# Second norm's scale and shift stored beside the x1 rows, a reordered end of attention, and useless matmuls in the waits of the routing

## The reference

```python
x = x + tanh(g_xattn) * attn(layernorm(x), ctx, Wq, bq, Wk, bk, Wv, bv)   # softmax(QK^T) * 256**-0.5 @ V
h = layernorm(x)                                     # the second norm
e = argmax(h @ router_w.T)                           # one expert for each token
x = x + tanh(g_ffn) * ((silu(h @ gate[e].T) * (h @ up[e].T)) @ down[e].T)
```

## Time and profile before

| | us |
|---|---|
| median of 3 runs | 225.41 |
| lowest and highest of them | 222.13, 226.23 |
| the profiled execution's own time | 221.01 |
| its span, first to last instruction | 218.9 |
| TensorE busy in the span | 199.7 (91%) |
| ScalarE, VectorE, GpSimd busy | 109.8, 130.8, 136.1 |
| mean granted TensorE clock, 1 is 2.4 GHz | 0.96 |

### The profile page before, as it was taken

One profiled execution on the slowest core, in us unless ns is written; L12 is line 12 of the kernel. 1 busy time (PEld: TensorE's weight loads), 2 busy tenths in 40 slices (PEclk: granted clock), 3 DMA queues, 4 the chain that ended last, 5 costly groups with the idle time before them and its releaser, 6 DMA issues.

```text
span 218.9 us, 4538 instructions
## 1 busy us (share of the span) xinstructions
PE 199.7 (91%) x1200; PEld 170.9 (78%) x1200; DVE 130.8 (60%) x430; ACT 109.8 (50%) x223; POOL 136.1 (62%) x138
## 2 busy tenths in 40 slices
PE   7899999997665789999999999999999999999960
PEld 3667998985564678888888888888888888888850
DVE  2886899867699125537555537564636565645650
ACT  1478777664500534495269485369475444422410
POOL 3004099495473897339966998987998985212111
PEclk9999999999787589999999999999999999999996
DMA  6999315928600319621581085194003012011000
GB/s 208 340 394 378 135 49 163 368 73 291 217 0 0 99 25 358 211 68 38 189 313 32 0 311 189 34 383 126 1 8 92 0 51 68 9 49 51 5 28 20
DMA packets 11845, 29.43 MB, mean 134 GB/s; under 512 B 1986, under 2 KB 8517, under 8 KB 10790
## 3 DMA queue, kind: packets, MB, share of 16 engines
q1 hardware_dynamic: 6320, 20.20, 25.9%
q0 software_dynamic: 2064, 5.12, 7.8%
q10 hardware_dynamic: 3430, 3.74, 5.1%
HBM read 24.85 MB, written 4.72 MB: 135 GB/s over the span
## 4 chain that ended last, share of the span: by engine, by line
PE 83%; DVE 6%; ACT 3%; DMA 3%; issue 2%; ACTq 1%; POOL 0%; POOLq 0%; DVEq 0%
PE ps L929 36%; PE ps L941 12%; PE ps L908 6%; PE ps L944 5%; PE ps L790 3%; PE ps L729 3%; PE ps L770 3%; DMA both<-in_ctxT 3%; PE ps L811 3%; PE ps L759 2%; PE ps L901 2%; PE ps L800 2%; PE ps L750 2%; PE ps L878 1%; DVE V L1193 1%
## 5 line engine op out<-in xcount | busy, mean ns | idle before, releaser
L929 PE MATMUL ps<-wgu,xhT 128*128 x360 | 83.1, 384 | 1.2 <-DVE xhT L1229 1.2
L929 PEld LDWEIGHTS ps<-wgu,xhT 128*128 128x128 f32 x360 | 66.3, 191 | 12.5 <-issue 1.6
L464 POOL DMA_INDIRECT xin<-x_rows,table x23 | 22.7, 986 | 29.4 <-DVE xin L1264 21.5
L941 PE MATMUL ps<-wd,hT 128*128 x114 | 40.5, 392 | 0.0
L396 POOL TENSOR_TENSOR wgu<-raw_gu,wgu (+1 forms) x12 | 38.6, 3253 | 0.1
L1246 DVE TENSOR_TENSOR A<-xin,ps 128x512 f32<-128x512 f32 (+1 forms) x40 | 20.6, 520 | 25.4 <-ACT xin L656 14.6
L656 ACT ACTIVATE xin<-ps 128x512 f32<-128x512 f32 (+1 forms) x40 | 18.6, 465 | 31.5 <-PE ps L929 31.1
L469 POOL DMA_INDIRECT out<-xin,table x20 | 20.3, 1015 | 18.3 <-DVE xin L1264 13.2
L650 ACT ACTIVATE hT<-ps 128x512 fp32r<-128x512 f32 x20 | 11.8, 592 | 32.9 <-PE ps L908 32.9
L944 PE MATMUL ps<-wd,hT 128*128 x95 | 26.6, 280 | 0.0
L941 PEld LDWEIGHTS ps<-wd,hT 128*128 128x128 f32 x114 | 21.3, 187 | 3.9
(11 more groups left out here) (163 smaller groups left out, 310.7 us busy)
## 6 DMA issues: line engine op xcount, KB each, us to landing
raw_gu<-in_Wgu SPq DMA_DIRECT2D x8, 1408.0 KB, 6.5
both<-in_Wd SPq DMA_DIRECT2D x8, 640.0 KB, 4.3
x_rows<-x ACTq DMA_DIRECT2D x8, 256.0 KB, 3.4
xin<-in_x SPq DMA_DIRECT2D x7, 256.0 KB, 8.8
both<-in_WdL SPq DMA_DIRECT2D x16, 64.0 KB, 4.7
both<-in_ctxT ACTq DMA_DIRECT2D x2, 480.0 KB, 7.1
xin<-x_rows,table POOLq DMA_INDIRECT x23, 3.6
out<-xin,table POOLq DMA_INDIRECT x20, 2.7
```

The costliest lines, as they stand in the source:

```text
L464: pool.indirect_dma_start(out=xg[:, j % SEATS, :], out_offset=None, in_=rows, in_offset=bass.IndirectOffsetOnAxis(ap=table[:, j:j + 1], ax ...
L929: last = pe.matmul(ps[:, g, 0:2 * WIDE if g < 2 else 4 * REST], xhT[:, j % 2, x_part, c, :], w, start=(c == 0 and (x_part, w_part) == (0, 0)),
L941: last = pe.matmul(ps[:, 6, 0:2 * H], hT[:, 0, c, :], wd[:, slot, c].rearrange("p o a n -> p (o a n)"), start=(c == 0), stop=(c == CI - 1) ...
```

## The change

1. `rows` becomes 258 wide: x1, scale, shift. `xin`, the input tile in SBUF, is 258 wide too; residual writes x1 back into it, and the buffer x1 goes. GpSimd makes scale and shift from start to end, in two parts: scales2(FIRST) for batches 0 to 2 between low_pieces(0) and low_pieces(1), scales2(LATER) for batches 3 to 7 behind low_pieces(1). Each is 16 small instructions in a row, each waiting for the one before.
2. The eight row DMAs on ScalarE's queue become two: FIRST (6 tiles) on ScalarE's queue in batch step 6 with the spare row behind it, LATER (10 tiles) on SyncE's queue behind load_d(2).
3. `r3`, `rem`, `weighed`, the 16 matmuls of L891 and `stat` go. ScalarE takes scale and shift from columns 256 and 257 of the gathered rows.
4. End of attention: TensorE's order in the last step becomes turn3(6), turn3(7), logits(6), logits(7); the last transposed x1 is copied to another place (last_x1T) and the last logits go to another bank, so neither waits for batch 6. VectorE makes route(6) behind statistics(7).
5. Counts: rounding up to whole tiles takes three instructions in place of four and a memset.
6. One-hots: `ohhi` and `uv` first, then 12 `ohlo` on VectorE, each raising v_lo; 4 `ohlo` and half of `uv` on ScalarE (activations Square, Relu and Copy), none on GpSimd.
7. Spins: 20 before the ranks, 64 behind them as before, 2 before each `ohlo` matmul, 72 in place of 24 behind the table, 12 behind turn_x(0).
8. The one-hot sum for `expert` is one reduction in place of a tree; two memsets move to the front; load_d(4) waits for t_tab in place of t_stat.

```diff
-SHARE = 3
+SHARE = 4
...
+FIRST, LATER = slice(0, 3 * TB), slice(3 * TB, NTOK)
...
             def load_d(e):
                 if e == SPLIT + 1:
-                    sp.wait_ge(t_stat, 1)
+                    sp.wait_ge(t_tab, 1)
...
                 arrived_gu(e)
                 if e:
                     load_d(e)
+                if e == SPLIT - 1:
+                    sp.wait_ge(p_st2, 2)
+                    sp.dma_start(rn[:, LATER], xin[:, LATER, :]).then_inc(d_row, 16)
                 arrived_d(e)
                 if e < SPLIT:
                     load_gu(e + RAW)
...
-            for e in range(SPLIT - 1):
-                low_pieces(e)
-
-            pool.wait_ge(v_guess, 1)
-            link(newton(pool, link, mv2[:, :, 0], rs2[:, 0, :], rs2[:, 1, :], ALL))
...
-            pool.wait_ge(v_slot, 1)
-            for t in range(NTOK - SHARE, NTOK):
-                ins = pool.tensor_scalar(ohlo[:, t, :], iota_lo[:], slot_f[:, 0, t:t + 1], None, ALU.is_equal)
...
+            def scales2(t):
+                pool.wait_ge(v_aggr, t.stop // TB)
+                link(guess(pool, link, mv2[:, t, 1], t))
+                newton(pool, link, mv2[:, t, 0], xin[:, t, H], xin[:, t, H + 1], t).then_inc(p_st2, 1)
+
+            low_pieces(0)
+            scales2(FIRST)
+            low_pieces(1)
+            scales2(LATER)
+
+            pool.wait_ge(d_row, 32)
             pool.wait_ge(d_zrow, 16)
             pool.wait_ge(v_tab, 1)
...  (ScalarE, batch loop)
                 turned2(i)
                 if i + 2 < B:
                     turned1(i + 2)
+                if i == B - 2:
+                    act.wait_ge(p_st2, 1)
+                    act.dma_start(rn[:, FIRST], xin[:, FIRST, :]).then_inc(d_row, 16)
+                    act.dma_start(rows[N:N + 1, :], xin[0:1, 0, :]).then_inc(d_zrow, 16)
                 if i:
-                    act.wait_ge(v_x1, i)
-                    act.dma_start(rv[i - 1], x1[:, (i - 1) % 2]).then_inc(d_row[(i - 1) % 2], 16)
                     turned3(i - 1)
...
             turned3(B - 1)
-            for step in range(B - 1, 3 * SPLIT):
+            split_first(B - 1)
+
+            act.wait_ge(v_slot, 1)
+            for t in range(SHARE):
+                if t == SHARE // 2:
+                    act.wait_ge(v_hi, 1)
+                    act.activation(uv[:, :, 1, :], ohhi[:], ACT.Copy, scale=iota_p[:, 0:1]).then_inc(a_uv, 1)
+                ins = act.activation(far[:, t, :], iota_lo[:], ACT.Square, scale=-1.0, bias=slot_f[:, 0, t:t + 1])
+            ins.then_inc(a_far, 1)
+            act.wait_ge(a_far, 1)
+            act.activation(ohlo[:, 0:SHARE, :], far[:], ACT.Relu, scale=-1.0, bias=one[:, 0:1]).then_inc(a_lo, 1)
+            for step in range(B, 3 * SPLIT):
                 split_first(step)
...
                 act.activation(xh[:, j % 2, :], seat(j), ACT.Identity,
-                               scale=stat[:, 0, j:j + 1], bias=stat[:, 1, j:j + 1]).then_inc(a_xh, 1)
+                               scale=scale_of(j), bias=shift_of(j)).then_inc(a_xh, 1)
...  (TensorE)
+                if i == B - 1:
+                    turn3(i)
                 if i:
                     logits(i - 1)
...
-            turn3(B - 1)
             logits(B - 1)
+            pe.wait_ge(a_x1T, B)
+            spin(20)
             pe.wait_ge(v_sort, 1)
...
             spin(64)
-            pe.wait_ge(v_lo, 1)
-            pe.wait_ge(p_lo, 1)
-            for t in range(NTOK):
+            pe.wait_ge(v_uv, 1)
+            pe.wait_ge(a_uv, 1)
+            for n, t in enumerate(list(range(SHARE, NTOK)) + list(range(SHARE))):
+                if t >= SHARE:
+                    pe.wait_ge(v_lo, t - SHARE + 1)
+                    spin(2)
+                else:
+                    pe.wait_ge(a_lo, 1)
                 last = pe.matmul(ps[:, 2, 0:2 * NT], ohlo[:, t, :], uv[:, t].rearrange("p a n -> p (a n)"),
-                                 start=(t == 0), stop=(t == NTOK - 1))
+                                 start=(n == 0), stop=(n == NTOK - 1))
             last.then_inc(t_tab, 1)
-            for t in range(NTOK):
-                if t % (NTOK // 2) == 0:
-                    pe.wait_ge(v_rsel, 2 * t // NTOK + 1)
-                last = pe.matmul(ps[:, 3, 0:6 * NT], ohlo[:, t, :], rsel[:, t]..., ...)
-            spin(24)
+            spin(72)
             pe.wait_ge(v_exp, 1)
...
             turn_x(0)
+            spin(12)
             every_tile(pe, "pe", tile, drain)
...  (VectorE)
-            link(dve.tensor_scalar(n_of, ps[...], 1.0, float(P - 1), ALU.max, ALU.add))
-            link(dve.tensor_copy(cnt_i[:, 0, :], n_of))
-            link(dve.tensor_scalar(cnt_i[:, 1, :], cnt_i[:, 0, :], 7, 7, ...shift_right, ...shift_left))
-            link(dve.tensor_copy(padded, cnt_i[:, 1, :]))
-            link(dve.memset(cnt[:, 4, :], 0.0))
+            link(dve.tensor_scalar(n_of, ps[...], 1.0, 1.0 / P, ALU.max, ALU.mult))
+            link(dve.tensor_scalar(cnt[:, 3, :], n_of, 255.0 / 512.0, BIG, ALU.add, ALU.add))
+            link(dve.tensor_scalar(padded, cnt[:, 3, :], -BIG, float(P), ALU.add, ALU.mult))
```

More of the change, by code:

```diff
@@ L133, in flamingo_moe @@
         turn = sb("turn", [P, NT], I32)
-        r3 = sb("r3", [P, NTOK, 3, 2], BF16)
-        stat = sb("stat", [P, 2, NT])
+        one = sb("one", [P, 1])
         table = sb("table", [P, NT], I32)
@@ L208, in flamingo_moe @@
         v_x1, v_aggr = sem("v_x1"), sem("v_aggr")
-        d_row = [sem("d_row0"), sem("d_row1")]
+        d_row = sem("d_row")
         d_zrow = sem("d_zrow")
@@ L372, in _ @@
                 lambda: pool.memset(mean_w, 1.0 / H),
+                lambda: pool.memset(one[:], 1.0),
             ]
@@ L810, in logits @@
                     for c in range(C):
-                        last = pe.matmul(ps[:, 5, E * k:E * k + E], x1T[:, c, P * k:P * k + P], wrc[:, c, :],
+                        last = pe.matmul(ps[:, LG_BANK(i), E * k:E * k + E], src[:, c, P * k:P * k + P], wrc[:, c, :],
                                          start=(c == 0), stop=(c == C - 1))
@@ L860, in _, with spin @@
                     router_mean()
-            turn3(B - 1)
             logits(B - 1)
+            def spin(n):
+                for _ in range(n):
+                    pe.matmul(ps[:, 1, 0:P], ones_b[:], tri[:], start=True, stop=True)
+            pe.wait_ge(a_x1T, B)
+            spin(20)
             pe.wait_ge(v_sort, 1)
@@ L873, in _ @@
             last.then_inc(t_rk, 1)
-            def spin(n):
-                for _ in range(n):
-                    pe.matmul(ps[:, 1, 0:P], ones_b[:], tri[:], start=True, stop=True)
             spin(64)
-            pe.wait_ge(v_lo, 1)
-            pe.wait_ge(p_lo, 1)
-            for t in range(NTOK):
+            pe.wait_ge(v_uv, 1)
[6 more added lines that the diff above has]
+                    pe.wait_ge(a_lo, 1)
                 last = pe.matmul(ps[:, 2, 0:2 * NT], ohlo[:, t, :], uv[:, t].rearrange("p a n -> p (a n)"),
-                                 start=(t == 0), stop=(t == NTOK - 1))
+                                 start=(n == 0), stop=(n == NTOK - 1))
             last.then_inc(t_tab, 1)
-            for t in range(NTOK):
-                if t % (NTOK // 2) == 0:
-                    pe.wait_ge(v_rsel, 2 * t // NTOK + 1)
-                last = pe.matmul(ps[:, 3, 0:6 * NT], ohlo[:, t, :], rsel[:, t].rearrange("p a n -> p (a n)"), start=(t == 0), stop=(t == NTOK - 1))
-            last.then_inc(t_stat, 1)
-            spin(24)
+            spin(72)
             pe.wait_ge(v_exp, 1)
@@ L1051, in _ @@
             link(measured(0, 2))
-            link(moments(FIRST))
-            scales(FIRST, link)
+            link(moments(EARLY))
+            scales(EARLY, link)
             def context(i):
@@ L1182, in _ @@
             dve.sem_inc(v_slot, 1)
[L1183 to L1198 removed]
+            dve.tensor_tensor(ohhi[:], iota_hi[:].to_broadcast([P, NTOK, NT]), slot_f[:, 1, :].unsqueeze(2).to_broadcast([P, NTOK, NT]),
+                              ALU.is_equal).then_inc(v_hi, 1)
+            dve.wait_ge(v_hi, 1)
+            dve.tensor_tensor(uv[:, :, 0, :], ohhi[:], iota_t[:].to_broadcast([P, NTOK, NT]), ALU.mult).then_inc(v_uv, 1)
+            for t in range(SHARE, NTOK):
+                dve.tensor_scalar(ohlo[:, t, :], iota_lo[:], slot_f[:, 0, t:t + 1], None, ALU.is_equal).then_inc(v_lo, 1)
             dve.wait_ge(t_tab, 1)
```

135 lines of the change are left out of this document (50 added, 85 removed).

## The result

| | before | changed |
|---|---|---|
| median of the runs, us | 223.62 (20 runs) | 226.30 (20 runs) |
| lowest and highest, us | 221.29, 226.53 | 222.71, 229.74 |
| the profiled execution's own time, its span, us | 221.01, 218.9 | 224.89, 222.5 |
| mean granted clock | 0.960 | 0.959 |

The ratio of the compared runs is 1.0093 [1.0053, 1.0132]: the change makes the kernel 1% slower, which is inside the 2% that the prediction counts as no change. Times of one kernel spread over some 3% here and a ratio takes only the runs near its fastest, so medians of all runs stand beside the ratios, and kernels are compared inside one series on one chip (the kernel before was at 223.6 to 225.4 from series to series).

What follows compares the result with a forecast made beforehand. TensorE has no gap before 50 us and behind 82; the routing between, and its clock, was what could be saved. Terms summed to -2.55 us; with another -0.85, the 225.4 median became 222.0, range 218.8 to 225.8.

Steps and rivals of the forecast that it cites:

- A: Mid-attention: scales2(FIRST) on GpSimd delays low_pieces(1), SyncE's load and ScalarE's split_first(6); +1.8 us, bounds 0 to 2.5.
- rival 2: End of attention: the clock falls in the hole GpSimd's chain makes, slowing ranks, logits and table; 224.5 on the median, chance 0.17.
- B: End of attention: turn3(7) ahead of logits(6), which fills the wait for ScalarE's copy; -0.95 us.
- C: Ahead of the ranks: spin(20) makes them wait 0.15 us longer, or 1.05 at half clock; +0.2 us taken.
- D: Counts: the cast in the middle and the memset go; -0.35 us.
- E: Slot numbers to table: 4.7 us in place of 5.6, -0.85; a table load for Square would cost 0.9.
- F: Table to first gathered tile: without weighed(1) on VectorE beside it the gather is earlier; 0 to -1.0, -0.5 us taken.
- G: Row DMA: LATER's 1290 KB take 6.2 us, land at 66.9, hidden before the table at 68.0; upper bound 3.2 late.
- rival 3: First gather: rows land late and the kernel ends slower, 226.0 on the median at the upper bound; chance 0.08.
- H: First transposes and up(0): spins keep TensorE dense at full clock; -0.3 at turn_x(0), -1.6 at up(0).
- rival 4: up(0): the spins don't hold the clock and it runs at half as before; 224.5 on the median, chance 0.10.
- Rival 1: Mid-attention: GpSimd's chain doesn't hold up ScalarE, so the sum is 1.8 us lower, 220.2 on the median; chance 0.15.

Runs made afterwards that it cites:

- the filled one: Changed kernel with 40 useless matmuls between turn2(7) and values(7), in the 2.5 us hole: 220.99 against 223.63 before; repeated in another series, 222.3 against 224.85.
- control of runs 6: The changed kernel once more, unedited, beside the runs with 40 useless matmuls in the hole: 226.13 against 223.63 before, ratio 1.009.
- the one with 1.77: Kernel before plus an idle chain of 16 GpSimd instructions between low_pieces(0) and low_pieces(1), leaving a 1.77 us hole: 228.51 against 224.14.
- runs 2 and 5: Changed kernel, FIRST's chain behind low_pieces(1): 222.98 against 223.66; both chains there, FIRST 14 tiles, LATER 2, old order at attention's end: 227.13 against 225.41.
- runs 2: Here the changed kernel with GpSimd's first chain moved behind low_pieces(1)'s gate and up, FIRST's DMA behind split_first(7): 222.98 against 223.66 before, ratio 0.999.
- runs 2 and 3: Changed kernel, FIRST's chain behind low_pieces(1): 222.98 against 223.66; both chains there, FIRST 14 tiles, LATER 2: 221.52 against 224.14, then 226.4 against 225.41.
- program of 3: Changed kernel with both GpSimd chains behind low_pieces(1), FIRST 14 tiles and LATER 2: 221.52 against 224.14 before, then 226.4 against 225.41 in another series.
- the last run: Changed kernel, both chains behind low_pieces(1), FIRST 14 tiles, 16 useless matmuls ahead of values(7), 20 ahead of ranks, 92 and 18 later: 222.01 against 224.85.

## Why the prediction was wrong

Forecast 222.0, measured 226.3, outside the range. By its steps:

- **A, right in size.** +1.8 forecast, 1.6 measured, with ScalarE's wait where it was looked for (1.51 us for 1.7).
- **The step that failed is that A is a plain delay.** The forecast "(A holds, clock full from the ranks on, rows in time)" had chance 0.50, and the sum put the clock lost in A's hole at nothing; rival 2 had 0.17. The mechanism of rival 2 is what happened, to the place (clock 0.50 from 58). Its price was wrong too: it counted 0.9 for the ranks, 0.3 for the logits and 0.5 to 1.3 for the table, some 2 us. Counted from values(7), the profile of the result is 2.9 us behind the filled one at up(0): 1.9 in values(7) to the last logits (6.65 us for 4.72), priced at 0.3, then 0.6 at the ranks and 0.5 up to the table. The control of runs 6, where the clock fell sooner, is 4.4 behind, 3.3 of them up to the last logits. At half clock these logits took 1.7 to 1.9 us for 1.06, the transposes 1.09 for 0.63. The row of the kernel before that should have warned is in the earlier trace rows: there the clock fell at 58, with TensorE standing for most of the three microseconds before. The place differs between executions, but the hole moves it: of the twelve profiles with 0.90 us unfilled ahead of values(7), two have the last logits at half clock (1.88 us) and three no fall there at all; all three with 2.5 us have it, and the one with 1.77.
- **B** is there where the clock is full (-0.8 in runs 2 and 5, -0.95 forecast) and buried where it isn't (+1.1: 6.65 us for 5.56).
- **C**: ranks 0.6 late at half clock (bound 1.05), 0.16 us of waiting at full clock.
- **D** -0.35 as said. **E** -1.3 in place of -0.85: matmuls every 0.16 us, no weighed(0) between, and ScalarE's share without a table load. The Trainium skill (ScalarE: Activation LUTs, Table sets: the hidden batching unit) names relu and copy as always there; the trace agrees, and shows the same of Square with this kernel's table.
- **F's reason fell.** Without weighed(1) beside it the first gather still starts 0.96 us behind the table (0.93 before) and takes 1.23 us for 1.35, and its tile is there 3.96 us behind the table for 4.20: a gain of 0.2, not 0.5. What holds the first gather back stays open. The Trainium skill (GPSIMD Engine Reference, Key points) has GpSimd and two-input VectorE instructions contend for SBUF; with weighed(1) gone the traces show no more than that 0.2 for it.
- **G**: landing in 6.3 us for 6.2, at 70.0, hidden in the changed kernel (table 72.85). Its slack was gone as soon as the chain moved (runs 2, gather 2.35 us behind the table): rival 3 waits behind rival 2.
- **H** -1.6 at up(0), right in the profile, but in a kernel that had already lost more than that by the clock. The pace of a spin was misread: the 52 of the earlier trace rows ran partly at half clock, and at full clock one takes 0.058 us (72 in 4.18), not 0.07. So spin(72) ended at 76.2 in the changed kernel, and TensorE stood 1.32 us before the first transposes; the clock held there, but not in the profiles of runs 2 and 3, where it stood 2.72 and 1.26.
- **The basis** was wrong: 4.4 us between the profiled execution and the median were partly put down to H (the "extra" -0.85). They were a lucky start of one execution and an unlucky median of 3 (225.41; later 223.6). Nor do the rivals carry that 0.85 alike: from 222.0, rival 3 would be 225.2 and rival 4 223.9. With the hole filled the medians are 2.6 us below the kernel before, and the sum without the 0.85 says 2.55; that they agree so well is luck in part, since E gave 0.45 more and F 0.3 less.

Rival 1 didn't happen (ScalarE's wait is in the rows), and rival 4 not in the changed kernel, where the spins held the clock up to up(0). In the profiles of runs 2 and 3 it did: up(0) took 5.18, 5.67 and 6.48 us.

The Trainium skill (TensorE: Matmul & The Clock Gate, HAM oscillation) has the clock lost in a wait between bursts. These traces agree as to the hole and the fall behind it or inside it; filled, the clock was kept through the logits in both profiles, and all the way to up(0) in one.

## What to carry to other kernels

Price a new hole on TensorE by what runs behind it at half clock, up to where the clock comes back, not by its own length: filling a hole of 2.5 us gave back 2.5 to 4.4 us here by the profiles and 5.1 by the medians, beside 1.6 us of plain delay that stayed. The mean clock does not show it (0.960 before, 0.959 changed): ask which work ran at half. If useless matmuls are to hold the clock, try the hole furthest ahead first; spins behind it can run at half clock themselves and then hold back ready work (0.6 us here). And look at the start of the profiled execution before reading its distance to the median as a hint on one stage.

## What the runs showed of the hardware that was not expected

- **How much one hole costs.** Filled, the granted clock read 1.00 through microseconds with TensorE at 0.53 and 0.69 busy. Not filled, the profile of the result has the hole of 2.5 us, a dense microsecond (56 to 57), then the fall, and the rise only ten microseconds later, with TensorE busy all the time from 58 on. The control has the fall inside the hole, before 54, and the rise at the same place, in 67 to 68.
- **The fall differs from one execution to the next.** The program of 3 was at half clock from 58 to 61.5 in one profile and at 1.00 there in the other; the filled kernel fell in 60 to 61 in one and not at all in the other. One profile does not give the price of a hole.
- **ScalarE stands 1.6 us longer in some executions.** Four of the eight profiles of the program of 3 and its variants (one of two of the very same program) have L654 2.15 to 2.4 us behind the activation before it in place of 0.6 to 0.85, with a releaser that is no engine of the core. The cause is open: an instruction transfer lies in the 4 us ahead of it in one of the four (the last run), and in none of the other three.
- **The start is chance.** The first score product began between 8.6 and 10.8 us and took 3.5 to 6.3 us, so it ended between 12.1 and 16.1; that can be a good part of the 3% between the runs of one kernel.
- **Rows in parts.** Over the profiles, stores of x1 rows of 1032 bytes landed in 4.3 to 5.2 us (774 KB), 6.0 to 6.7 (1290 KB) and 7.7 to 8.5 (1806 KB), and 3.1 to 5.2 (258 KB beside the big one).
